# Rebuilding the first three steps of a cross-attention and FP4 feed-forward kernel: order of work on five engines

## The reference

```python
n   = layernorm(x)
k,v = split((ctx @ Wsrc.T + b) * mask);  q = (n @ Wtgt.T + b) * mask
att = softmax(where(mask == 0, -inf, q k / 4)) v            # 8 heads of 16
x   = x + concat(n, att) @ Wout.T + b_out
h   = silu(fp4(m) @ fp4(w_gate).T) * (fp4(m) @ fp4(w_up).T)  # m = layernorm(x), 352 wide
x   = x + fp4(h) @ fp4(w_down).T
```

## Time and profile before

| | before |
|---|---|
| median of 3 runs | 195.42 us (195.29 to 196.22) |
| the profiled execution | 195.18 us |
| its span, first to last instruction | 193.0 us |
| TensorE busy | 183.4 us (95%) |
| VectorE busy | 178.9 us (93%) |
| GpSimd busy | 138.2 us (72%) |
| ScalarE busy | 130.2 us (67%) |
| granted TensorE clock | 1.00 of full speed |
| loaded and stored | 11.99 MB, mean 62 GB/s |

### The profile page before, as it was taken

How to read it: one execution, slowest core, us unless ns; L and a number is a source line. 1 busy time by engine, 2 the same in 40 slices (tenths; PEclk the granted TensorE clock), 3 DMA queues, 4 the chain that set the end, 5 groups by cost and what they waited for, 6 DMA issues and landing times.

```text
span 193.0 us, 5839 instructions
## 1 busy us (share of the span) xinstructions
PE 183.4 (95%) x2098; PEld 141.7 (73%) x2098; DVE 178.9 (93%) x402; ACT 130.2 (67%) x277; POOL 138.2 (72%) x205
## 2 busy tenths in 40 slices
PE   7799989999999999999999999899999999899985
PEld 7574857859768698597786776566777886677884
DVE  6679999899999999999988999999999999999992
ACT  3507889869779698796968845475565673666761
POOL 6333595576698897984928489697999985776770
PEclk9999999999999999999999999999999999999999
DMA  5799239450120000000000000000101010101005
GB/s 187 257 270 371 79 104 288 163 165 0 23 94 0 3 3 3 2 0 5 3 3 0 3 2 0 0 2 5 54 0 58 0 54 0 54 5 56 0 3 163
DMA packets 13698, 11.99 MB, mean 62 GB/s; under 512 B 790, under 2 KB 10590, under 8 KB 13670
## 3 DMA queue, kind: packets, MB, share of 16 engines
q1 hardware_dynamic: 13086, 11.23, 18.6%
q10 hardware_dynamic: 584, 0.39, 0.6%
HBM read 9.52 MB, written 2.10 MB: 60 GB/s over the span
## 4 chain that ended last, share of the span: by engine, by line
PE 40%; POOL 32%; issue 14%; DVE 7%; DMA 3%; ACT 2%; POOLq 1%; ACTq 0%; DVEq 0%
POOL wq_y L404 10%; POOL hq L419 8%; PE bank L1124 6%; PE bank L1112 5%; POOL sch L411 3%; PE bank L1075 3%; PE a_pair L1075 3%; PE bank L1087 3%; PE bank L1118 3%; DMA wsT<-in_WsT 3%; POOL xn L291 2%; PE bank L1061 2%; PE bank L1133 2%; PE bank L1134 2%; PE bank L1097 2%
## 5 line engine op out<-in xcount | busy, mean ns | idle before, releaser
L1215 PE MATMUL bank<-wdT,hT 128*128 128x128 f32 x186 | 26.2, 277 | 1.7 <-issue 1.6
L1180 PE MATMUL bank<-guT,xqT 128*128 128x352 f32 x64 | 24.7, 468 | 1.0 <-DVE hh L910 0.9
L1215 PEld LDWEIGHTS bank<-wdT,hT 128*128 128x128 f32 x186 | 23.2, 191 | 2.6 <-issue 2.3
L1183 PE MATMUL bank<-guT,xqT 128*128 128x352 f32 x64 | 24.2, 459 | 0.0
L404 POOL TENSOR_TENSOR wq_y<-hh,ivh 128x704 f32<-128x704 f32 x15 | 21.2, 1411 | 3.0 <-ACT ivh L651 2.4
L419 POOL TENSOR_TENSOR hq<-wq_u,sch 128x704 f32<-128x704 f32 x14 | 19.4, 1388 | 4.6 <-DVE wq_u L936 4.5
L757 DVE TENSOR_REDUCE den<-prob 128x8 f32<-128x512 f32 x32 | 19.7, 664 | 0.0
L645 ACT COPY hT<-bank 128x384 f32<-128x384 f32 x32 | 15.2, 474 | 4.1 <-PE bank L1195 4.1
L632 ACT ACTIVATE a_pair<-wq_y 128x704 f32<-128x704 f32 x15 | 11.5, 765 | 8.8 <-DVE wq_u L936 7.4
L526 ACT ACTIVATE k_bd<-bank,bk_of,head_of 128x512 f32<-128x512 f32 x15 | 11.9, 803 | 7.9 <-PE bank L1112 7.9
L1183 PEld LDWEIGHTS bank<-guT,xqT 128*128 128x128 f32 x64 | 12.1, 190 | 6.8 <-ACT mask_bc L566 0.2
(11 more groups left out here) (144 smaller groups left out, 507.4 us busy)
## 6 DMA issues: line engine op xcount, KB each, us to landing
cT<-in_ctxT SPq DMA_DIRECT2D x8, 512.0 KB, 6.1
x_all<-in_x SPq DMA_DIRECT2D x8, 256.0 KB, 6.7
mask_bc<-in_mask_rows SPq DMA_DIRECT2D x8, 256.0 KB, 6.7
out_y<-mask_bc SPq DMA_DIRECT2D x7, 256.0 KB, 2.2
wsT<-in_WsT ACTq DMA_DIRECT2D x1, 256.0 KB, 4.9
out_y<-x_all SPq DMA_DIRECT2D x1, 192.0 KB, 2.0
w_all<-in_wg SPq DMA_DIRECT2D x1, 176.0 KB
w_all<-in_wu SPq DMA_DIRECT2D x1, 176.0 KB
```

Of the source, the lines that this page charges most:

```text
L1180: nc.tensor.matmul(gu_bank[2 * n % 3][:, 0:I], xqT[g % 2][:, t], guT[:, 0, :], start=True, stop=True).then_inc(pe_g, 1)
L1183: nc.tensor.matmul(gu_bank[(2 * n + 1) % 3][:, 0:I], xqT[g % 2][:, t], guT[:, 1, :], start=True, stop=True).then_inc(pe_u, 1)
L1215: last = nc.tensor.matmul(bank[:, j * P:(j + 1) * P], hT[n % 2][:, c, :], wdT[:, c, :], start=(c == 0), stop=(c == 2))
```

## The change

- **Group 0 in halves.** Two transposes go to the first half of w0, two to o_bank. Copying, query projection and masking are done a half at a time. All 18 warm-ups go. `v_project(0, 0)`, half of group 0's values, moves from step 1 into step 0, ahead of the query halves, and group 0's values go to av_bank.
- **Score masks.** The large `neg_mask` (groups 1 to 7) goes from GpSimd to ScalarE (`masks()`, at the head of its step 1).
- **Maxima.** For group 0, TensorE subtracts all four maxima, so VectorE's subtraction goes. In step 1 TensorE issues them earlier, and the transposes of probabilities 0 and 1 are placed around them. ScalarE does `exp(0, 0)` and `exp(0, 1)` earlier, ahead of `k_evac(1, 0)`.
- **Step 1 on VectorE.** `normalise1(1)` stands between the second and the third row maximum; `weights_maxima` moves behind `q_masked(1)` and `stats1(2)`.
- **Step 2.** `stats1(3)` moves from VectorE's step 1 to its step 2, ahead of `weights_round_up(0)` and `q_masked(2)`. `rstd1_of(3)` moves from GpSimd's step 1 to its step 2, behind `expand_reciprocals(1)`. `spread_reciprocals(0)` moves on TensorE behind group 2's transposes and key projection.
- **Loads.** SyncE waits for the end of group 0's query projection (`pe_q`) before it issues the feed-forward weights and everything behind them.

```diff
@@ SyncE
             sp.wait_ge(w_zero, 2)
+            sp.wait_ge(pe_q, 1)
             for r, w in ((0, wg), (1, wu)):
@@ GpSimd
             rstd1_only(1)
-            pool.wait_ge(ld_mb, 16 * PAIRS)
-            pool.wait_ge(mb_zero, 2)
-            nc.gpsimd.tensor_scalar(neg_mask[:, TILES:, :], mask_b[:, TILES:, :], BIG, -BIG,
-                                    ALU.mult, ALU.add).then_inc(nm_ok, 1)
...
                 if k == 1:
                     add_bias(0)
                     add_bias(1)
+                if k == 2:
                     rstd1_of(3)
                 if on(g1 + 2) and k > 1:
                     rstd1_of(g1 + 2)
@@ ScalarE
+            def masks():
+                act.wait_ge(ld_mb, 16 * PAIRS)
+                act.wait_ge(mb_zero, 2)
+                nc.scalar.activation(neg_mask[:, TILES:, :], mask_b[:, TILES:, :], ACT.Copy, bias=-BIG, scale=BIG
+                                     ).then_inc(nm_rest, 1)
...
+                if k == 1:
+                    masks()
                 if on(g2):
                     v_evac(g2)
...
+                if k == 1:
+                    exp(0, 0)
                 if on(g1) and k > 0:
                     xnT_evac(g1)
+                    if k == 1:
+                        exp(0, 1)
@@ VectorE
             normalise1(0)
-            dve.wait_ge(pe_xnT, 1)
-            nc.vector.tensor_copy(xnT[0][:, :], w0[:, :]).then_inc(xnT_ok, 1)
+            for h in range(2):
+                dve.wait_ge(pe_xnT if h else pe_xh, 1)
+                nc.vector.tensor_copy(xnT[0][:, halves[h]], half_bank[h][:, 0:GT // 2]).then_inc(xnT_ok if h else xh_ok, 1)
+            dve.wait_ge(ld_m[0], 16)
+            dve.wait_ge(ld_b, 16)
+            for h in range(2):
+                dve.wait_ge(pe_q if h else pe_qh, 1)
+                nc.vector.scalar_tensor_tensor(out=q_m[0][:, halves[h]], in0=half_bank[h][:, 0:GT // 2], scalar=b_q,
+                                               in1=mask_bc[:, halves[h]],
+                                               op0=ALU.add, op1=ALU.mult).then_inc(qm_ok if h else qh_ok, 1)
...
                     for p in range(PAIRS):
                         row_max(g2, p)
-                if k == 1:
-                    normalise1(1)
+                        if k == 1 and p == 1:
+                            normalise1(1)
                 if on(g3):
                     update(g3)
-                if on(g2) and k < NG:
+                if on(g2) and 1 < k < NG:
                     minus_max(g2)
...
                 if k == 1:
-                    weights_maxima()
                     k_block(1, 1)
                 if k == 2:
+                    stats1(3)
                     weights_round_up(0)
-                if on(g1):
+                if on(g1) and k > 0:
                     q_masked(g1)
                 if k < 2:
                     stats1(k + 1)
                 if k == 1:
+                    weights_maxima()
                     weights_scales()
...
-                    stats1(3)
@@ TensorE
+            def first_transpose(h):
+                pe.wait_ge(xn_ok, 1)
+                for j in range(2):
+                    last = nc.tensor.transpose(half_bank[h][:, j * P:(j + 1) * P], xn[0][:, 2 * h + j, :], ident[:, :])
+                last.then_inc(pe_xnT if h else pe_xh, 1)
+
+            def first_queries(h):
+                pe.wait_ge(ld_wt, 16)
+                pe.wait_ge(xnT_ok if h else xh_ok, 1)
+                nc.tensor.matmul(half_bank[h][:, 0:GT // 2], wtT[:, :], xnT[0][:, halves[h]],
+                                 start=True, stop=True).then_inc(pe_q if h else pe_qh, 1)
...
                 if k == 1:
-                    v_project(0, 0)
                     v_project(0, 1)
                     k_project(1)
                 if on(g3):
                     attend(g3)
+                if on(g3) and k > 2:
                     spread_reciprocals(g3)
+                if k == 1:
+                    minus_max(0, 0)
+                    minus_max(0, 1)
                 if k == 0:
                     k_project(0)
-                    xn_transpose(0)
-                    warm_up(8)
-                    q_project(0)
-                    warm_up(10)
+                    first_transpose(0)
+                    first_transpose(1)
+                    v_project(0, 0)
+                    first_queries(0)
+                    first_queries(1)
...
+                if k == 2:
+                    spread_reciprocals(0)
-                if on(g2):
+                if on(g2) and k > 1:
                     minus_max(g2, 0)
                     minus_max(g2, 1)
                 if k == 1:
+                    prob_transpose(0, 0)
+                    minus_max(0, 2)
+                    minus_max(0, SUB)
                     bias_of_values()
                 if on(g1) and k > 0:
                     q_project(g1)
-                if on(g2):
+                if k == 1:
+                    prob_transpose(0, 1)
+                if on(g2) and k > 1:
                     minus_max(g2, 2)
```

More of the change, by code:

```diff
@@ L46, in on, with subtractions @@
     return 0 <= g < NG
+def subtractions(g, p):
+    return g * SUB + (1 if g > 0 else 0) + p + 1
 def evacuations():
@@ L182, in xattn_ffn @@
         calm_ok = sem("calm_ok")
+        nm_rest = sem("nm_rest")
+        pe_xh, xh_ok, pe_qh, qh_ok = sem("pe_xh"), sem("xh_ok"), sem("pe_qh"), sem("qh_ok")
+        halves, half_bank = (slice(0, GT // 2), slice(GT // 2, GT)), (w0, o_bank)
         up_tile_ok, round_tile_ok = sem("up_tile_ok"), sem("round_tile_ok")
@@ L504, in v_evac @@
                 act.wait_ge(v_zero, 2)
-                vp = w0[:, :].rearrange("r (t p e d) -> r t p e d", t=TILES, p=PAIRS, e=2)
+                vp = (w0 if g > 0 else av_bank)[:, :].rearrange("r (t p e d) -> r t p e d", t=TILES, p=PAIRS, e=2)
                 for b in range(2):
@@ L532, in exp @@
                 pr = prob[g % 2][p][:, :, :].rearrange("p j c -> p (j c)")
-                if p == SUB and g < NG - 1:
-                    act.wait_ge(sub_ok, g + 1)
+                if p == SUB and 0 < g < NG - 1:
+                    act.wait_ge(sub_ok, g)
                     nc.scalar.activation(pr, pr, ACT.Exp, scale=float(HD) ** -0.5).then_inc(p_ok, 1)
                     return
-                act.wait_ge(pe_mm, g * SUB + p + 1)
+                act.wait_ge(pe_mm, subtractions(g, p))
                 past(act, pe_T, n + 1 - 2 * PAIRS)
@@ L607, in attn_step @@
                 if on(g2):
-                    exp(g2, 0)
-                    exp(g2, 1)
+                    if k > 1:
+                        exp(g2, 0)
+                        exp(g2, 1)
                     exp(g2, 2)
@@ L727, in q_masked @@
                 dve.wait_ge(ld_m[g], 16)
-                if g == 0:
-                    dve.wait_ge(ld_b, 16)
                 past(dve, pe_s, g - 1)
@@ L737, in row_max @@
                 dve.wait_ge(pe_s, g + 1)
-                past(dve, *((sub_ok, g) if p == SUB else (pe_mm, (g - 1) * SUB + p + 1)))
+                if g > 0:
+                    dve.wait_ge(*((sub_ok, g - 1) if p == SUB and g > 1 else (pe_mm, subtractions(g - 1, p))))
                 nc.vector.tensor_reduce(mx[p][:, :, :].rearrange("r j e -> r (j e)"),
@@ L1045, in scores @@
                 s = g % 2
-                pe.wait_ge(nm_ok, 1 if g == 0 else 2)
+                pe.wait_ge(*((nm_ok, 1) if g == 0 else (nm_rest, 1)))
                 pe.wait_ge(c_sel, PAIRS - 1)
@@ L1101, in xn_transpose @@
                 pe.wait_ge(xn_ok, g + 1)
-                past(pe, v_ok, g)
+                past(pe, v_ok, g if g > 1 else 0)
                 for j in range(TILES):
@@ L1120, in v_project @@
             def v_project(g, half):
-                pe.wait_ge(qm_ok, g + 1)
+                bank = w0 if g > 0 else av_bank
+                if g > 0:
+                    pe.wait_ge(qm_ok, g + 1)
                 for j in (2 * half, 2 * half + 1):
                     for c in range(2):
-                        last = nc.tensor.matmul(w0[:, j * P:(j + 1) * P], cT[g % 4][:, c, j * P:(j + 1) * P],
+                        last = nc.tensor.matmul(bank[:, j * P:(j + 1) * P], cT[g % 4][:, c, j * P:(j + 1) * P],
                                                 wsT[:, c, D:2 * D], start=(c == 0), stop=(c == 1))
```

2 lines of the change are left out of this document (added).

## The result

The changed kernel takes 199.5 us in the median (197.5 to 200.5, 4 runs) against 195.35 for the kernel before beside it (4 runs): a ratio of 1.017, 95% interval 1.013 to 1.022. The forecast was 196.2 with a range to 197.4, so both the point and the range missed. Measured again it took 200.5 (200.2 to 200.7, 4 runs; ratio 1.025, 1.022 to 1.029).

A forecast was written before the change was run, and what follows sets the result against it. TensorE's gapless work from 36 to 97 us was taken to carry start shifts to the end: 0.45 and 0.65 won, 0.65 and 1.2 lost, so 195.42 + 0.75 = 196.2 us, range 194.7 to 197.4.

The forecast's parts named there:

- SyncE's new wait: Loads on SyncE's queue held until about 10.4 us; b_out taken to land at 16.5, before bias_of_values at 16.7: no cost.
- the bias loads are late: Rival: b_out lands at 18.7, adding 1.7 us to everything from group 1's masked queries; 197.9 us; chance 0.13.
- q2: Start of the second group's masked queries on VectorE; forecast 18.3 against 19.42 before, 1.1 us earlier.
- T3: Start of TensorE's transposes in step 3; 39.26 before, forecast 40.0, a shift of +0.75 us.
- Front in halves: Step 0: group 0 in halves ends query masking at 10.9 instead of 11.36, gaining 0.45 us.
- `masks()` at nothing: ScalarE, step 1: the mask work, at most 2.1 us, costs zero, its rows landing by 10.3 and work done at 12.4.
- VectorE's list in step 2: From second to third group's masked queries: 1.52 us of weights_maxima and 0.25 of wait added; third starts at 30.95, 0.5 later.
- GpSimd as the decisive place: Step 2: rstd1_of(3), taken as 1.9 us behind group 1's reciprocals, delays normalise1(3) and step 3's transposes; 1.2 us lost.
- One-for-one carry: Whatever the start wins or loses by step 3's transposes reaches the end unchanged, without slack in steps 3 to 7.
- The clock: TensorE stays at full clock; rival: 1.2 GHz in gaps left by dropped warm-ups doubles about 3 us, 199; chance 0.03.
- GpSimd in time: Rival, step 2: group 1's reciprocals come a microsecond earlier, step 3's transposes wait for nobody; shift -0.45, 195.0; chance 0.16.
- the gain is kept: Rival, step 1: VectorE's 1.5 us idle before k_block(1, 1) is absent; 1.1 or more carried, 194.2; chance 0.12.

The follow-up runs named there:

- the exchange: Changed kernel with b_out's load reading 128 different rows of another 64 KB matrix instead of one row 128 times: 198.4 us, ratio 1.015.
- before with late rstd: Kernel before with only stats1(3) and rstd1_of(3) moved to step 2 as in the change: 196.3 us, ratio 1.003.
- without the two waits: Changed kernel without SyncE's wait for pe_q and with rstd1_of(3) ahead of expand_reciprocals(1): 195.9 us, ratio 1.003.
- `start_kept`: Kernel before plus group 0's halves, early values, maxima on TensorE, earlier normalise1(1) and exponentials; GpSimd's large mask held behind normalise1(1): 196.0 us, ratio 1.001.
- with the spread back: Changed kernel without pe_q wait, rstd1_of(3) ahead of expand_reciprocals(1), and weights_maxima, GpSimd's large mask and spread_reciprocals(0) in old places: 196.25 us, ratio 1.005.
- `start_kept` with the bias loads early: `start_kept` with the loads of woT and b_out issued before SyncE's wait for the cleared feed-forward weights: 195.0 us, ratio 0.999.

## Why the prediction was wrong, point by point

The step that failed is "SyncE's new wait". It took the landing of b_out as 16.5, hidden; it was 19.5. The forecast had two ends, 15.9 and 18.7, and its rival "the bias loads are late" is what happened, with 0.13 of the chances. Two readings were wrong in it. The old 5.3 us were taken for queueing that a late issue gets back. It got nothing back: woT's transfer, just ahead in the queue, fell from 6.6 to 2.7 us, b_out's from 5.3 to 5.1, and 2.1 of that hang on its one source row, as the exchange shows (3.0 against 5.1). And the rival's issue at 13.4 was 14.44, since one issue of x ahead of it held SyncE 1.70 us; six issues at 0.5 left no room for that. Hence +2.65 at q2 where the rival said +1.7.

Against the forecast's own times the 4.26 at T3 is:

| term | forecast | measured | off by |
|---|---|---|---|
| q2 start | 18.3 | 20.95 | +2.65 |
| q2 to q3 | 12.65 | 12.83 | +0.18 |
| q3 to reciprocals | 3.15 | 3.15 | 0 |
| reciprocals to `rstd1_of(3)` | 0.95 | 1.12 | +0.17 |
| `rstd1_of(3)` | 1.9 | 2.25 | +0.35 |
| its end to T3 | 3.05 | 3.22 | +0.17 |

Together 3.52, and 0.75 + 3.52 is the 4.26 with rounding.

Against the kernel before, q2 is 1.53 later, q2 to q3 takes 1.79 more, and q3 to T3 0.94 more.

- **Front in halves: right.** Masked queries were done at 10.88 (forecast 10.9), step 1's transposes began at 15.26 (15.2), VectorE waited 1.95 for ScalarE's key block (1.5).
- **`masks()` at nothing: wrong in its reason, almost right in this execution.** It ended at 13.62 and cost the value copies little. But its rows came at 11.9 here, not by 10.3, and at 13.6 and 14.15 elsewhere; the bound of 14.01 from the earlier trace rows was a fair one and should have stood in the range as a delay.
- **VectorE's list in step 2: right**, within 0.2, with 0.20 of wait for the spread reciprocals (forecast 0.25). But two things hold step 2 about equally long here: with `weights_maxima` taken out again it is still 12.82. Only with the spread in its old place too is it 11.03 (before: 11.04).
- **GpSimd as the decisive place: right in mechanism, mis-sized.** Its wait, ScalarE's wait behind it (2.65) and TensorE's (1.59, by ScalarE's values) are all as drawn. Put on before alone it costs 1.0. The term is 2.25, over my 1.9 and its bound of 2.08: the second instruction took 0.73 where it takes 0.20 in the next set. In VectorE's timeline `wq_u` begins 0.02 after it and ends with it, and it reads two inputs from SBUF:

```profile
38.34 0.66 DVE L841 SCALAR_TENSOR_TENSOR wq_u<-wq_a,wq_y 128x512 f32<-128x512 f32 x1
```

The same 0.73 to 0.74 is in the repeat and in before with late rstd. The Trainium skill ("SBUF — State Buffer", "Who interferes with whom") has a VectorE instruction with two SBUF inputs contend with a GpSimd instruction that reads SBUF; by that rule the forecast had 2.5 for the chain. The trace agrees in kind and lies between that and what I took. For the length of such an instruction the forecast used the 0.74 of q_masked, which reads one of its two tensors from a matmul bank; `wq_u` takes 0.66.
- **One-for-one carry: right.** T3 + 4.26, last matmuls 194.05 against 189.68, + 4.37. The span grew by 4.7. That the median grew by 4.15 is less of a match than it looks: the four spans are 195.6, 195.7, 197.7 and 198.3, and the profiled one is of the long ones.
- **The clock: as forecast in the profiled execution**, 1.00 in every stretch, though TensorE was idle up to 2.6 us. Not in all: its mean was 0.991 in one of the other three, and 0.99 in three of the four of the repeat. It isn't needed for the 4.26. Where a trace shows the fall, it stands behind the wait for b_out, which the forecast didn't have, and not in the gaps of the dropped warm-ups.
- **"GpSimd in time" and "the gain is kept": out.** Even without the two waits the gain would not have been kept, since step 2 is 1.8 longer: with `weights_maxima` moved back, TensorE's late spread holds VectorE 1.86 us. In the changed kernel that work covers it (0.20).

What stays open: why two of the changed kernel's four executions have spans 2 us shorter than the profiled one, and why the clock falls behind some waits for b_out and not behind others. And the time around the span is 2.1 to 2.2 us in every execution of before, but 1.9 to 3.6 in the changed kernel, 2.1 to 4.1 in `start_kept` and 2.4 to 3.9 with the spread back. Five spare semaphores didn't bring it about, and it was 2.0 to 2.3 in `start_kept` with the bias loads early, on another chip. I have no cause for it.

## What to carry to other kernels

A wait put ahead of a queue of loads delays all of them (here the first by 4.4 us and b_out by 3.9): find the first consumer of each load behind it, take the landing time from issue as it stands, and call it queueing only if another execution or row shows the same transfer faster. When a start is made faster, look first at the loads that just made it before. Here the saving of the halves reached the median only once a 64 KB load was issued 6 to 7 us earlier. When work is taken out of a list and its length stays (12.82 both times), something else held it just as long: look for the wait that grew. Don't queue a short step with ready inputs behind one that waits: moving four instructions ahead of it brought step 3's transposes 1.5 us forward.

## What the runs showed of the hardware

- A load of 64 KB in which 128 partitions read one 512-byte row takes longer than one that reads 128 rows: 4.8 to 5.1 us against 3.0, issued at the same place in the same queue. Elsewhere the same load took 4.7 to 6.5, and 7.4 to 10.0 when it was issued at 4.4 to 6.4 us.
- A transfer's issue on SyncE took between 0.33 and 3.0 us in the first 20 us of these kernels: woT's took 2.02 in before, 2.50 in the changed kernel without the wait, and 0.51 in the changed kernel, where SyncE had paused from 3.9 to 10.4. Six such issues can't be priced at the shortest.
- The key mask's rows let `masks()` begin anywhere from 10.1 to 14.15 in kernels that issue them alike.
- A GpSimd instruction on 128x1792 values and VectorE's normalisation of 128x128 tiles got in each other's way: one VectorE instruction took 1.82 us beside it, 0.34 otherwise.
- The granted clock fell to the 1.2 GHz level behind TensorE waits of 2.06 and 2.35 us in two profiled executions, and stayed at full behind waits of 2.56 and 2.58 in two others. The fall cost 0.6 and 0.9 us between the bias matmuls and q2.
